# The up projection of a six-layer transformer as three fp32r products, with W1 staged in the buffer of the QKV weights

## The reference

```python
xn = (x - mu) / jnp.sqrt(var + 1e-05) * g + bln
hg = xn @ W1 + b1                      # 128 -> 2 x 341
a, gate = jnp.split(hg, 2, -1)
return a * jax.nn.gelu(gate, approximate=False) @ W2 + b2
```

## Time and profile before

| What | Value |
|---|---|
| Runs, median (lowest to highest) | 1501.54 us (1500.04 to 1501.63) |
| Profiled execution: its span, the only time it has of its own | 1500.0 us |
| Mean granted TensorE clock | 0.995 |
| PE busy | 98% of the span |
| DVE, ACT, POOL busy | 87%, 85%, 83% |

### The profile page before, as it was taken

The page is one execution under the profiler, slowest core; times in us unless marked ns, Lnnn a source line. Parts: engine busy times, 40 slices in busy tenths (PEclk is TensorE's granted clock), DMA queues, the critical chain, the costliest instruction groups (busy, mean ns, idle before and its releaser), DMA issues.

```text
span 1500.0 us, 66306 instructions
## 1 busy us (share of the span) xinstructions
PE 1464.2 (98%) x26320; PEld 1280.8 (85%) x26320; DVE 1310.1 (87%) x2365; ACT 1267.7 (85%) x2551; POOL 1248.7 (83%) x1213
## 2 busy tenths in 40 slices
PE   6799999999999999999999999999999999999997
PEld 5578888888888888888888888888888888888886
DVE  6799998889889898888898898889898988998974
ACT  4578888889888888888898888888888888888886
POOL 5489988888888888888888888888888888888781
PEclk9899999999999999999999999999999999999999
DMA  6012212111212111121211121211112121112111
GB/s 185 22 46 60 59 46 57 43 49 42 59 49 79 52 47 43 54 63 52 70 41 50 43 70 49 69 45 50 47 40 55 52 54 38 49 35 52 38 49 39
DMA packets 96184, 80.28 MB, mean 54 GB/s; under 512 B 66282, under 2 KB 79598, under 8 KB 95854
## 3 DMA queue, kind: packets, MB, share of 16 engines
q1 hardware_dynamic: 94990, 75.34, 18.8%
q10 hardware_dynamic: 864, 0.26, 0.1%
HBM read 17.91 MB, written 1.05 MB: 13 GB/s over the span
## 4 chain that ended last, share of the span: by engine, by line
PE 93%; issue 2%; DVE 2%; POOL 1%; ACT 1%; DMA 0%; ACTq 0%; DVEq 0%; POOLq 0%
PE bank L1065 74%; PE bank L1179 11%; PE bank L1217 6%; PE bank L1251 1%; PE bank L1149 1%; DMA rot<-in_b_v 0%; POOL rot L459 0%; DVE parts L891 0%; DVE newton L910 0%; DVE s L937 0%; DVE n L901 0%; DVE am L825 0%; POOL w_lo L446 0%; ACTq L550 0%; ACT rot L576 0%
## 5 line engine op out<-in xcount | busy, mean ns | idle before, releaser
L459 POOL TENSOR_TENSOR rot<-parts 128x512 f32<-128x512 f32 x384 | 493.3, 1285 | 120.4 <-DVE parts L891 120.3
L891 DVE TENSOR_TENSOR parts<-bank,rtab 128x1024 f32<-128x1024 f32 x384 | 459.8, 1208 | 0.4 <-POOL rot L459 0.3
L470 POOL TENSOR_TENSOR rot<-rot,rnorm 128x512 f32<-128x512 f32 x384 | 391.1, 1046 | 10.0 <-DVE rnorm L917 10.0
L901 DVE TENSOR_REDUCE n<-sq 128x8 f32<-128x512 f32 x384 | 257.7, 671 | 33.0 <-ACT sq L627 33.0
L689 ACT ACTIVATE pz<-bank 64x512 f32<-64x512 f32 x384 | 226.1, 589 | 61.4 <-PE bank L1217 59.1
L1065 PE MATMUL bank<-w_hi,x_hi 128*128 128x512 f32 x576 | 263.8, 458 | 4.6 <-DVE parts L891 3.6
L476 POOL TENSOR_TENSOR es<-es,r 128x512 f32<-128x512 f32 x192 | 202.6, 1055 | 75.2 <-DVE r L943 75.2
L627 ACT ACTIVATE sq<-bank 128x512 f32<-128x512 f32 x384 | 230.4, 601 | 28.0 <-DVE n L901 22.0
L1065 PE MATMUL bank<-w_hi,x_lo 128*128 128x512 f32 x576 | 229.5, 398 | 0.0
L1065 PE MATMUL bank<-w_lo,x_hi 128*128 128x512 f32 x576 | 229.1, 398 | 0.0
L1179 PE MATMUL bank<-ident,rot 128*128 128x128 f32 x1536 | 203.1, 275 | 5.0 <-POOL rot L470 2.4
(11 more groups left out here) (86 smaller groups left out, 2660.4 us busy)
## 6 DMA issues: line engine op xcount, KB each, us to landing
vb<-v SPq DMA_DIRECT2D x96, 384.0 KB, 3.8
w_new<-in_Wqkv SPq DMA_DIRECT2D x36, 256.0 KB, 4.2
vb<-v SPq DMA_DIRECT2D x48, 128.0 KB, 3.4
w_o<-in_Wo SPq DMA_DIRECT2D x12, 256.0 KB
xin<-x_tok SPq DMA_DIRECT2D x48, 64.0 KB, 2.1
xs<-x_tok SPq DMA_DIRECT2D x48, 64.0 KB, 2.0
xin<-x_tok SPq DMA_DIRECT2D x48, 56.0 KB, 2.7
xs<-x_tok SPq DMA_DIRECT2D x48, 56.0 KB, 2.0
```

What stands on the lines that cost most here:

```text
L459: g.tensor_tensor(rot[:, i * CH:(i + 1) * CH].rearrange(halves, z=2, c=HD), parts[:, b:b + CH].rearrange(halves, z=2, c=HD), parts[:, b + ...
L470: g.tensor_tensor(c, c, over(r, CHH, DH), ALU.mult).then_inc(s_sc[i], 1)
L891: d.tensor_tensor(parts[:, b:b + 2 * CH].rearrange("p (w h c) -> p w h c", w=2, c=DH), heads(bank[QK_BANK[i]][:, :]).unsqueeze(1).to_broad ...
L901: d.tensor_reduce(n2[:, T * 2 * HEADS + m * CHH:T * 2 * HEADS + (m + 1) * CHH], heads(sq[:, b:b + CH]), op=ALU.add, axis=AX.X).then_inc(s_ ...
```

## The change

The up projection becomes three fp32r products like those of QKV. w_1 is gone; W1 comes into the first 682 columns of w_new, ACT splits off w1_hi and DVE w1_lo (for layer 0, POOL), one buffer each. xg becomes xg_hi and xg_lo: ACT writes xg_hi (fp32r) in `affine`, then writes the same values in full to the second half of bank 0 in `affine2`, and DVE subtracts the one from the other in `xg_lo_part`, which raises s_xg. Loads into w_new are reordered to make room for W1, the weight splits of Wqkv run one iteration earlier (SPLIT_FROM), and waits that `freed` writes are adapted; the order of the other work is as before. maskf moves into es, and the semaphores s_ve0 and s_rbase are merged into others. Cut to its core:

```diff
-WLOADS = 7
+WLOADS = 6
-SPLIT_FROM = 2
+SPLIT_FROM = 1
-        w_1 = sb("w_1", 2 * 2 * HID)
+        w1_hi = sb("w1_hi", 2 * HID, F32R)
+        w1_lo = sb("w1_lo", 2 * HID, F32R)
...
             def qkv_weights(l, c):
                 sp.wait_ge(s_wl, max(0, (l - 1) * WCH + c + 1))
+                if c < 2 and l != 2:
+                    sp.wait_ge(s_upl, max(0, l - 1) if l > 1 else l)
...
+            def up_weights(l):
+
+                if l < DEPTH - 1:
+                    sp.wait_ge(s_wl, (l + 1) * WCH + 2 if l else 2)
+                else:
+                    sp.wait_ge(s_upl, l)
+                sp.dma_start(w_new[:, 0:2 * HID], W1[l * P:(l + 1) * P, :]).then_inc(s_up, 16)
...
+            up_weights(0)
-            for c in range(WCH):
+            for c in (2, 3, 4, 5, 0, 1):
                 qkv_weights(1, c)
...
+            def first_up_lo():
+                pool.wait_ge(s_uph, 1)
+                g.tensor_tensor(w1_lo[:, :], w_new[:, 0:2 * HID], w1_hi[:, :].bitcast(F32), ALU.subtract)\
+                 .then_inc(s_upl, 1)
...
+            def split_up(l):
+                act.wait_ge(s_up, 16 * (l + 1))
+                for j in range(HCH):
+                    act.wait_ge(s_hid[j], l * SEQS)
+                a.activation(w1_hi[:, :], w_new[:, 0:2 * HID], ACT.Copy).then_inc(s_uph, 1)
...
+                act.wait_ge(s_xg, n)
                 l = layer(n)
-                a.activation(xg[:, :], bank[N_BANK][:, 0:LEN], ACT.Identity, bias=shift[:, l:l + 1],
-                             scale=gain[:, l:l + 1]).then_inc(s_xg, 1)
+                a.activation(xg_hi[:, :], bank[N_BANK][:, 0:LEN], ACT.Identity, bias=shift[:, l:l + 1],
+                             scale=gain[:, l:l + 1]).then_inc(s_xgh, 1)
+
+            def affine2(n):
+                l = layer(n)
+                act.wait_ge(s_xnt, done(n))
+                a.activation(bank[N_BANK][:, LEN:2 * LEN], bank[N_BANK][:, 0:LEN], ACT.Identity, bias=shift[:, l:l + 1],
+                             scale=gain[:, l:l + 1]).then_inc(s_xgf, 1)
...
                     gelu(n - 5, 0)
                     exp_and_log()
+                    up_hi(n - 5)
...
                     affine(n - 4)
+                    affine2(n - 4)
...
+            def xg_lo_part(n):
+                dve.wait_ge(s_xgh, done(n))
+                dve.wait_ge(s_xgf, done(n))
+                d.tensor_tensor(xg_lo[:, :], bank[N_BANK][:, LEN:2 * LEN], xg_hi[:, :].bitcast(F32), ALU.subtract)\
+                 .then_inc(s_xg, 1)
...
                     middle(n - 3, 1)
+                if live(n - 5):
+                    up_lo(n - 5)
...
                     stats(n - 3)
+                if live(n - 4):
+                    xg_lo_part(n - 4)
                 if live(n):
                     rotate(n, 1)
...
             def hidden(n, j):
 
                 pe.wait_ge(s_xg, done(n))
+                if n % SEQS == 0:
+                    pe.wait_ge(s_upl, layer(n) + 1)
                 for half in range(2):
-                    w = (par(n) * 2 + half) * HID + j * P
-                    last = mm(bank[H_BANK[j]][0:width(j), half * LEN:(half + 1) * LEN], w_1[:, w:w + width(j)], xg[:, :])
+                    w = slice(half * HID + j * P, half * HID + j * P + width(j))
+                    o = bank[H_BANK[j]][0:width(j), half * LEN:(half + 1) * LEN]
+                    mm(o, w1_hi[:, w], xg_hi[:, :], stop=False)
+                    mm(o, w1_lo[:, w], xg_hi[:, :], start=False, stop=False)
+                    last = mm(o, w1_hi[:, w], xg_lo[:, :], start=False)
                 last.then_inc(s_hid[j], 1)
```

More of the change, by code:

```diff
@@ L124, in program @@
         xn = sb("xn", TILES * P)
-        xg = sb("xg", LEN)
+        xg_hi = sb("xg_hi", LEN, F32R)
+        xg_lo = sb("xg_lo", LEN, F32R)
         gt = sb("gt", HCH * LEN)
@@ L145, in program @@
         rbase = gt[:, 0:4 * TILES * DH]
+        maskf = es[:, 0:4 * 64]
         abq = sb("abq", 2)
@@ L213, in program @@
         s_xnt = sem("s_xnt")
+        s_xgh = sem("s_xgh")
+        s_xgf = sem("s_xgf")
         s_xg = sem("s_xg")
+        s_up = sem("s_up")
+        s_uph = sem("s_uph")
+        s_upl = sem("s_upl")
         s_hid = sems("s_hid", HCH)
@@ L281, in _ @@
                 sp.dma_start(dst, src).then_inc(s_table, 16)
-            sp.dma_start(maskf[:, :], masks).then_inc(s_late, 16)
+            sp.dma_start(maskf, masks).then_inc(s_late, 16)
             def weights(l, part):
@@ L292, in weights @@
                                  Wo[r:r + half * P, :].rearrange("(a p) c -> p a c", p=P)).then_inc(s_w, 16)
[L293 to L296, removed]
+                elif part < 5:
+                    j = part - 2
                     rows = width(j)
@@ L369, in later_weights @@
                     sp.wait_ge(s_xready, n)
-                for part in ((0,), (1,), (2,), (3, 4), (5, 6), (), (), ())[k]:
+                for part in ((0,), (1,), (2, 3), (4, 5), (), (), (), ())[k]:
                     weights(l, part)
             def later_qkv(n):
[L375 to L379, removed]
+                l, k = n // SEQS, n % SEQS
+                if k == 2 and l > 0:
+                    up_weights(l)
+                for c in ((), (), (), (2,), (3,), (4,), (5, 0), (1,))[k]:
+                    if l + 2 < DEPTH:
+                        qkv_weights(l + 2, c)
+            sp.wait_ge(s_zero, 3)
             def iteration(n):
@@ L440, in _ @@
                                            rb[:, k, T, :].unsqueeze(1).to_broadcast([P, DEPTH, DH]), ALU.mult)
-            last.then_inc(s_rbase, 1)
+            last.then_inc(s_zero, 1)
             def split_lo(l, c):
@@ L606, in next_hi, with up_hi @@
                     split_hi(layer(n) + 1, c)
+            def split_up(l):
[3 more added lines that the diff above has]
+                a.activation(w1_hi[:, :], w_new[:, 0:2 * HID], ACT.Copy).then_inc(s_uph, 1)
+            def up_hi(n):
+                if n % SEQS == SEQS - 1 and layer(n) < DEPTH - 1:
+                    split_up(layer(n) + 1)
             for s in range(-1, SEQS + 1):
@@ L961, in moments, with up_lo @@
                     d.bn_aggr(mv[:, T * 2:(T + 1) * 2], stat[:, T * 6:(T + 1) * 6]).then_inc(s_mv, 1)
+            def xg_lo_part(n):
[3 more added lines that the diff above has]
+                 .then_inc(s_xg, 1)
+            def up_lo(n):
+                if n % SEQS == SEQS - 1 and layer(n) < DEPTH - 1:
+                    dve.wait_ge(s_uph, layer(n) + 2)
+                    d.tensor_tensor(w1_lo[:, :], w_new[:, 0:2 * HID], w1_hi[:, :].bitcast(F32), ALU.subtract)\
+                     .then_inc(s_upl, 1)
             def gated(n, j):
@@ L1284, in iteration @@
                 if live(n - 3):
-                    freed((s_sub[1], n - 2, 4, 1), (s_qte[3], n - 2), (s_xready, n - 6))
+                    freed((s_sub[1], n - 2, 4, 1), (s_xready, n - 6), (s_mid[1], n - 4))
                     values(n - 3, 2)
-                    freed((s_rot[0], n - 1, 8, 2), (s_xg, n - 5))
+                    freed((s_rot[0], n - 1, 8, 2), (s_xg, n - 5), (s_rot[1], n - 2, 8, 7), (s_ot[3], n - 4))
                     values(n - 3, 3)
@@ L1298, in iteration @@
                 if live(n - 5):
[L1299 to L1304, removed]
+                    freed((s_qte[6], n - 2), (s_pte[1], n - 3, 4, 3), (s_hm[1], n - 6))
                     hidden(n - 5, 1)
@@ L1309, in iteration @@
                     scores(n - 2, 1)
[L1310 removed]
+                    freed((s_rot[0], n - 1, 8, 4), (s_pte[0], n - 3, 4, 2), (s_qte[1], n - 2))
                     turn_p(n - 2, 0)
@@ L1314, in iteration @@
                 if live(n - 5):
[L1315 to L1319, removed]
+                    freed((s_mid[0], n - 3), (s_hm[2], n - 6))
                     hidden(n - 5, 2)
-                    freed((s_ot[3], n - 3), (s_rot[0], n - 1, 8, 2), (s_xg, n - 5))
+                    freed((s_ot[3], n - 3), (s_xg, n - 5))
                     hidden(n - 5, 0)
@@ L1366, in iteration @@
                 if live(n - 4):
-                    freed((s_rot[1], n - 1, 8, 7), (s_hm[0], n - 5))
+                    freed((s_rot[1], n - 1, 8, 7), (s_hm[0], n - 5), (s_ot[3], n - 3))
                     turn_normal(n - 4)
@@ L1375, in iteration @@
                 if live(n - 2):
-                    freed((s_qte[1], n - 1), (s_rot[0], n - 1, 8, 6), (s_pte[0], n - 2, 4, 0))
+                    freed((s_qte[1], n - 1), (s_pte[0], n - 2, 4, 0))
                     turn_p(n - 2, 2)
```

48 lines of the change are left out of this document (21 added, 27 removed).

## The result

The change costs 6%: 1590.95 us (median of four runs, 1589.6 to 1592.4) against 1501.17 beside it, a ratio of 1.0595 with a 95% interval of 1.0582 to 1.0609. The forecast was 1601, in a range of 1563 to 1650. The profiled execution has a span of 1590.6 us, 90.6 more than before.

The account below looks back on a forecast made before the run. It took PE, busy 98% of the span, as the bound. From 1500.0 us: -23 product, +92 stall, +5 weights, +2 start, +1 draining, +24 clock = 1601 us, range 1563 to 1650.

Parts of the forecast that it names:

- Product, 48 steps: On PE, 18 fp32r matmuls of 0.117 us replace 12 fp32 products a step: 0.48 us gained each, 23 us in all.
- Stall at project(n, 2): PE waits for s_xg, now raised late in DVE's list, before writing bank 0: 2.1 us, 44 times, +92 us.
- Layer edges: W1's splitting on ACT and DVE once a layer delays xg_lo_part: 1 us, 5 times, +5 us (0 to 10).
- Clock in the steady part: Stalls lower PE's clock in one iteration of three: 15 falls of 1.6 us, +24 us (0 to 70).
- Start, draining, their clock: At the start, load_x(0) on SP queues behind loads awaiting POOL's split, +2 us (0 to 5); draining adds +1.
- POOL's hold: DVE's newton_root waits for POOL's add, so its later start is swallowed; stats start 0 to 0.46 us later.
- Rival 3: On PE, fp32r matmuls of 256 columns take 0.23 us, as at 512: 1674 us, chance 0.05.
- Rival 1: The same stall of PE, but its clock stays up: 1577 us, low end 1568, chance 0.33.
- rival 2: PE's clock falls in nearly every iteration: 1647 us, chance 0.10.
- The sign that was promised for it: In the profile after, PE's granted clock would be under 1.00 in many of the 40 slices.
- Draining: At the end, the longer way from layer norm to xg_lo counts once or twice: +1 us.
- Rival 4: xg_lo_part ends by 712.8, in DVE's idle time before squares, so PE never waits: 1485 us, chance 0.04.

Follow-up runs that it names:

- e3: Kernel before, fp32 products kept, with affine2 on ACT and an unused DVE subtraction ahead of s_xg: 1603.07 us, ratio 1.0672.
- e5: The changed kernel with one more ACT operation of affine2's shape, into an unused buffer, between affine and affine2: 1627.94 us, ratio 1.0838.
- e9: The changed kernel with POOL's add(n, 0) moved behind scale(n - 1, 4): 1580.22 us, ratio 1.0522.
- e10: e6 with POOL's add(n, 0) moved behind scale(n - 1, 4): 1547.23 us, ratio 1.0304.
- e4: The changed kernel with affine2 writing to an SBUF buffer instead of bank 0, so project(n, 2) waits only for affine2: 1493.63 us, ratio 0.9946.
- e7: e4 with xg_lo_part ahead of stats(n - 3) in DVE's list: 1488.36 us, ratio 0.9909.
- e8: e7 with the loads of chunks 0 and 1 of layer 1 moved behind load_x(0) on SP: 1484.86 us, ratio 0.9886.
- e1: The changed kernel with xg_lo_part moved ahead of squares(n, 1) in DVE's list: 1505.4 us, ratio 1.0025.
- e2: The changed kernel with xg_lo_part between squares(n, 1) and newton_root in DVE's list: 1550.33 us, ratio 1.0321.
- e6: The changed kernel with only the hi x hi product in the up projection, all splits kept: 1599.09 us, ratio 1.0639.

## Why the prediction was right, and where its sizes were off

It fell in the range, with the forecast's mechanism, 10 us too high. By its steps, of the 90.6 us between the two spans:

| Step | Forecast | Measured |
|---|---|---|
| Product, 48 steps | -23 | -25 (0.52 a step, e3 against the change) |
| Stall at project(n, 2) | +92 (2.1 us, 44 times) | +91 (2.01 us in the median, 44 times) |
| Layer edges | +5 | +1.5 (0.58 us, 5 times, less the 1.4 that the longer stalls there hold) |
| Clock in the steady part | +24 (15 falls of 1.6) | +10 (8 falls of 1.2) |
| Start, draining, their clock | +3 | +13 (the rest to 90.6) |

That the total is so near is in part luck: the clock was put 14 us too high, start and draining together 10 us too low.

**The stall** was right in place, size and number, by its own steps: affine2 took the 0.46 us to the next start, DVE's squares were late by as much, and POOL's hold swallowed part of it. That reading, of one row only, was the weakest link, and e5, e9 and e10 bear it out: in these three traces the 36 or 37 newton_roots that found POOL idle took 0.17 to 0.18 us each, while in the change all 96 found POOL at work and ended 0.05 us behind its instruction, whether they took 0.24 us or 1.26. The Trainium skill ("SBUF — State Buffer", section "Who interferes with whom") says that a DVE instruction with two SBUF inputs and a GpSimd instruction that reads SBUF contend, and that the second to issue is blocked until the first is done. The traces agree: e4's subtraction out of SBUF, issued behind POOL's scaling, took 1.15 us and ended behind it, and in e7, issued ahead of it, 0.41.

**The product** was taken 0.002 us too short for each matmul; its gain, put at 0.48 us a step, is 0.47 by the rows and 0.52 by the periods of e3. Rival 3, fp32r at 256 columns as slow as at 512, is refuted by the 0.119 us.

**The clock** is the term that was mis-sized. Both the number of falls (15 against 8) and the price (1.6 against 1.2 us) were too high. The price of 1.6 took it that PE works through all of the slow stretch and that nothing of it is won back; the periods with a fall are 1.2 us longer. In the stretch shown above, 782.90 to 786.40, PE did work throughout, but not all of its work took twice as long: the 128 short matmuls of the scores took 1.98 us to the next row's start in place of 1.39. Twice the time would have cost 0.4 us more, which is the difference of 1.6 and 1.2. PE's timeline, one period earlier at 2.4 GHz and then in that stretch:

```profile
752.34 1.46 PE L1126 MATMUL bank<-kt,qt 64*32 64x64 f32 x128
753.73 0.50 PE L1126 MATMUL bank<-w_hi,x_hi 128*128 128x512 f32 x1
...
783.70 2.05 PE L1126 MATMUL bank<-kt,qt 64*32 64x64 f32 x128
785.68 0.79 PE L1126 MATMUL bank<-w_hi,x_hi 128*128 128x512 f32 x1
```

The rule of the Trainium skill ("TensorE: Matmul & The Clock Gate", section "HAM oscillation") that only longer gaps lower the clock, which the prediction named, did not hold in the steady part: falls followed stalls eight times, six of 2.01 to 2.08 us and two of 2.29. Rival 1 (no fall) and rival 2 (one in nearly every iteration) bracket what came. The sign that was promised for it, many of the 40 slices under 1.00, was a bad one: a fall of 3.4 us does not bring a slice of 40 us under 0.9, and the digits are the same 9 as without it.

**Draining** was put at +1, against 11.1 for that stretch as a whole, of which 2.1 are the last of the 44 stalls; by its share no step was further off. The text counted a longer way from layer norm to xg_lo, and did not look at DVE's list there: xg_lo stands behind stats of the next step, which wait for a transfer. Taking xg_lo ahead of stats brought 1.4 us of it back (e7 against e4). Of the 11.1 us, PE's idle time makes 6.4 and its busy time 4.6. The second part is the clock, less what the products save: it was at 1.2 GHz for the last 22.6 us, where before it fell only at 1497.5, behind PE's last matmul. e4 has the same products and the same wait of 3.46 us, but the lower clock for 3.4 us only while PE still had work, and there PE was busy 5.8 us less. Why the clock stayed low in the change is open.

**The start**: PE's first take_in of the layers came at 52.9 us in place of 51.3, +1.6 against a forecast of +2, by the mechanism named, two loads queued ahead of load_x(0). With them moved, e8 has it at 51.6, and reaches the 6th at 171.1 in place of 173.9 (e7). In the change, the rest of the 4.1 us ahead of the 6th take_in holds the first stall, 2.85 us, and a clock that was at 1.2 GHz for 24 us there, where it had been for 14.

**Rival 4**, faster with the signal in time, is what e4, e7 and e8 are. Its estimate of 1485 comes out in e8, which mends the start and the draining too, and in e7 to 3 us; the place it named, DVE's idle time ahead of squares, gave e1 its 1505: there the move of xg_lo alone takes away all but 0.34 us of the stall.

## What to carry to other kernels

Before a buffer gets a reader on another engine, follow the release of that buffer, not the work of the reader: here two operations that hid in their engines' idle time turned 0.7 us of room into 2 us of stall, because the signal moved into the middle of another engine's fixed list. A gain on the engine that bounds is worth its time only while no loop through the other engines is longer; the cheapest repair is a buffer whose release does not hang on the late engine (e4, 97 us for 1 KB a partition), and then the order inside that engine's list. Count the draining and the start by the lists as well, since what is late there is not what is late in the steady part.

## What the runs showed that was not expected

- **How often the clock falls goes with the length of the stall, but not evenly.** Periods of the steady part with a fall, of 42, by the usual stall: none at 1.38 us (e2), 4 and 2 at 1.87 (e9, e10), 2 and 8 at 2.00 and 2.01 (e3 and the change), 17 at 2.33 (e5), 20 at 2.66 (e6). In e9 and e10 all six falls came behind the longer stall of a layer edge, 2.28 or 2.29 us; none of the 70 stalls of 1.87 in the two traces was followed by one. e3 and the change have the same usual stall and differ fourfold, though only two of the change's eight came behind a layer edge; what else decides was not tried, and each count is of one execution.
- **Less work on PE made the kernel slower**: e6 at 1599.1 us, with a third of the up projection, against 1590.95 with all of it. Its period at the full clock is level (30.99 against 31.05), and the falls of the clock, 20 against 8, make its steady part 15 us longer.
- **Two instructions of other engines, in a place where neither is the bound, are worth 11 us**: e9 moves one add of POOL's behind one scaling, and takes 0.14 us from each of 42 periods, and in the one trace of each half of the falls (4 in place of 8).
